# The down projection of pairs 2 and 3 in seven products over all eight pieces, with the last two pieces' sums kept among the token operands

## The reference

```python
xn = layernorm(x)
q, k, v = (xn @ W.T + b for each)              # 512 -> 512
kv_sum = cumsum((elu(k) + 1) * v, axis=1)
s = ((elu(q) + 1) * kv_sum * SCALE) @ Wo.T + bo
y = fwht(xn * SU_ug) / 64                      # Walsh-Hadamard transforms
hid = silu(y @ W_gate.T * ws_gate) * (y @ W_up.T * ws_up)     # 512 -> 2048
g = silu((fwht(hid * SU_dp) / 64) @ W_down.T * ws_down)       # 2048 -> 512
out = x + s * g
```

## Time and profile before

| | us |
|---|---|
| median of 3 runs | 1291.22 (1289.54 to 1293.17) |
| the profiled execution's own time | 1291.18 |
| its span, first to last instruction | 1289.4 |
| PE busy | 1259.5 (98%) |
| DVE busy | 936.1 (73%) |
| ACT busy | 618.3 (48%) |
| POOL busy | 108.9 (8%) |

### The profile page before, as it was taken

One profiled execution on the slowest core, in us unless ns is written; L12 is line 12 of the kernel. 1 busy time (PEld: TensorE's weight loads), 2 busy tenths in 40 slices (PEclk: granted clock), 3 DMA queues, 4 the chain that ended last, 5 costly groups with the idle time before them and its releaser, 6 DMA issues.

```text
span 1289.4 us, 16166 instructions
## 1 busy us (share of the span) xinstructions
PE 1259.5 (98%) x5896; PEld 570.7 (44%) x5896; DVE 936.1 (73%) x1417; ACT 618.3 (48%) x912; POOL 108.9 (8%) x159
## 2 busy tenths in 40 slices
PE   5999999999999999999999999999999999999998
PEld 3544444444444444444444444444444444444443
DVE  6989989878656777777883778776773767775724
ACT  5894655532245655552334555554233655454212
POOL 1000001131210000120022001000001000000001
PEclk9999999999999999999999999999999999999999
DMA  9534775777757356575378333323526433332423
GB/s 370 224 131 125 242 215 186 241 251 292 229 205 237 113 196 231 220 251 196 131 229 257 134 128 134 131 99 103 205 93 196 145 117 116 113 129 76 130 95 103
DMA packets 65472, 226.21 MB, mean 175 GB/s; under 512 B 7408, under 2 KB 17904, under 8 KB 50800
## 3 DMA queue, kind: packets, MB, share of 16 engines
q1 hardware_dynamic: 41840, 170.64, 36.7%
q0 software_dynamic: 16272, 42.48, 11.9%
q10 hardware_dynamic: 7280, 12.06, 2.7%
HBM read 171.64 MB, written 53.50 MB: 175 GB/s over the span
## 4 chain that ended last, share of the span: by engine, by line
PE 78%; DVE 9%; issue 5%; ACT 5%; DMA 3%; SPq 0%; DVEq 0%; ACTq 0%
PE bank L2450 40%; PE bank L2636 13%; PE bank L2330 12%; PE bank L2516 7%; PE bank L2541 2%; PE bank L2661 2%; ACT work L1229 1%; ACT work L1232 1%; DMA h_all<-scr_f 1%; DVE work L1675 1%; PE bank L2375 1%; PE bank L2561 1%; DVE work L1659 1%; DVE work L1665 1%; DVE work L1702 1%
## 5 line engine op out<-in xcount | busy, mean ns | idle before, releaser
L2450 PE MATMUL bank<-xops,ring 128*128 128x512 f16 x2772 | 603.2, 379 | 7.4 <-DVE work L1702 2.6
L2450 PEld LDWEIGHTS bank<-xops,ring 128*128 128x128 f16 x2772 | 269.4, 98 | 340.2 <-issue 11.1
L2330 PE MATMUL bank<-xops,ring 128*128 128x512 f16 x1008 | 225.2, 379 | 0.5 <-DVE ring L1831 0.5
L1212 ACT ACTIVATE work<-bank 128x512 f32<-128x512 f32 x198 | 117.8, 595 | 214.7 <-PE bank L2450 200.2
L1659 DVE TENSOR_TENSOR work<-bank,work 128x512 f32<-128x512 f32 x198 | 133.4, 686 | 113.0 <-PE bank L2450 99.8
L2636 PE MATMUL bank<-h_all,ring 128*128 128x512 f16 x768 | 166.8, 379 | 0.2 <-DVE work L1659 0.2
L2330 PEld LDWEIGHTS bank<-xops,ring 128*128 128x128 f16 x1008 | 98.1, 98 | 123.6 <-issue 9.1
L2636 PEld LDWEIGHTS bank<-h_all,ring 128*128 128x128 f16 x768 | 75.0, 98 | 91.0 <-DVE work L1659 0.7
L1259 ACT ACTIVATE h_all<-work 128x512 f16<-128x512 f32 x116 | 70.6, 624 | 62.6 <-DVE work L1702 62.5
L1711 DVE TENSOR_TENSOR h_all<-work,h_all 128x512 f16<-128x512 f32 x116 | 79.3, 686 | 5.7 <-ACT h_all L1259 4.4
L1665 DVE SCALAR_TENSOR_TENSOR work<-work 128x512 f32<-128x512 f32 x64 | 44.1, 690 | 51.2 <-ACT work L1232 50.8
(11 more groups left out here) (284 smaller groups left out, 1323.4 us busy)
## 6 DMA issues: line engine op xcount, KB each, us to landing
ring<-scr_g SPq DMA_DIRECT2D x72, 1024.0 KB, 4.8
ring<-scr_d SPq DMA_DIRECT2D x15, 1024.0 KB, 5.8
scr_g<-ring SPq DMA_DIRECT2D x22, 512.0 KB, 4.4
h_all<-in_ug_t SPq DMA_DIRECT2D x8, 1024.0 KB, 12.9
ring<-in_down_t SPq DMA_DIRECT2D x6, 1024.0 KB, 6.5
scr_g<-ring POOLq DMA_DIRECT2D x12, 512.0 KB, 5.7
work<-in_x_t SPq DMA_DIRECT2D x6, 1024.0 KB, 7.0
scr_g<-h_all POOLq DMA_DIRECT2D x12, 512.0 KB, 2.9
```

The lines of the kernel that those rows point to most:

```text
L1212: act.activation(tile(g, j), chain_bank(g)[:, :], ACT.Copy).then_inc(copied, 1)
L2330: mm = pe.matmul(plain_bank(g, j)[:, :], at[:, s, 2 * dh + kk, r, :], xops[:, kk, xs, PLAIN_B[dh][c], :], start=(n == 0), stop=(n == len(t ...
L2450: mm = pe.matmul(to[:, :], weight_of(slot, s, b, kk), at, start=(a == 0 and m in (P1, P2, P5)), stop=(a == 5), skip_group_check=True)
```

## The change

SEVEN becomes 8: `seven` goes over all eight pieces, and `rest` goes, with its products, banks, weights and additions. In numbers of instructions for each of the pairs 2 and 3: the down product had 7 x 2 x 18 + 4 x 2 x 12 = 348 matmuls and has 7 x 2 x 24 = 336. The order of its products is now P1, P2, P6, P7, P4, P5, P3, both halves of each in turn, so P1 of the second half now stands ahead of both halves of P2, and P4 ahead of P5.

T2, T3 and T4 of pieces 6 and 7 have no home left; they go to the token operands `xops`, in the places of T2 and T3 (and of B21 for T4), once the last up group has used them (P2 for piece 6, P7 for piece 7). They are written by two instructions, of 1024 and of 512 columns. Pair 3's tokens come into `xops` later, since `x_high(3, 0)` now also waits for P4 of both halves. `load_x(3)` also waits for piece 7's sums. The token preparation of pair 3 on ACT and DVE is cut up and mixed with silus and additions. Two more units (6 and 7) are made in pair 1. There is one weight slot less to load in each pair (seven loads of 1 MB for eight).

In the diff `hidden_sums_high`, `x_high` and the first `seven_and_o` are ACT's, the second `seven_and_o` and `last_sums` DVE's, `seven` is PE's; IN_RES is 6.

```diff
-SEVEN_FROM, SEVEN = 2, 6
-DOWN_SLOTS = (P1, P2, P6, P7, P5, R11, P4, P3)
+SEVEN_FROM, SEVEN = 2, FP
+DOWN_SLOTS = (P1, P2, P6, P7, P4, P5, P3)
+DOWN_ORDER = [(d, m) for m in DOWN_SLOTS for d in range(2)]
-GATE_ORDER = [(d, j) for j in (C11, C22, C21, C12) for d in range(2)]
+GATE_ORDER = [(d, j) for j in (C11, C21, C22, C12) for d in range(2)]
...
+        def homes_late(i, s):
+            b = (T2, T3)[i - IN_RES]
+            return xops[:, :, s, b, :], xops[:, i - IN_RES, s, B21, :]
...
             def load_x(p):
                 sp.wait_ge(h_ready, 32 * p)
+                if p > SEVEN_FROM:
+                    sp.wait_ge(hidden_sums_ready, sums_of_hidden(p - 1, SEVEN - 1))
...
             def load_last_res():
+                sp.wait_ge(seven_done, down_to(PAIRS - 1, 1, P5))
...
             def x_high(p, kk):
                         act.wait_ge(product_done, products_to(p - 1, GROUPS - 1, P3))
+                        act.wait_ge(seven_done, down_to(p - 1, 1, P4))
...
             def hidden_sums_high(p, i):
+                act.wait_ge(product_done, products_to(p, GROUPS - 1, (P2, P7)[i - IN_RES]))
+                two, third = homes_late(i, HI)
+                act.activation(two, work[:, at:at + 2, :], ACT.Copy)
+                act.activation(third, work[:, at + 2, :], ACT.Copy).then_inc(hidden_sums_hi, 1)
...
             def seven_and_o(p):
-                if p < PAIRS - 1:
-                    x_high(p + 1, 0)
-                    t_high(p + 1, 0)
-                    x_high(p + 1, 1)
-                    t_high(p + 1, 1)
                 for d, j in GATE_ORDER:
+                    if p < PAIRS - 1:
+                        if (d, j) == (0, C21):
+                            x_high(p + 1, 0)
+                        elif (d, j) == (0, C22):
+                            t_high(p + 1, 0)
+                            x_high(p + 1, 1)
+                        elif (d, j) == (0, C12):
+                            t_high(p + 1, 1)
                     seven_gate(p, d, j)
...
             def seven_and_o(p):
+                for d in range(2):
+                    seven_add(p, d, "11")
                 if p < PAIRS - 1:
                     x_sums(p + 1, 0)
                     t_low(p + 1, 0)
-                for d in range(2):
-                    seven_add(p, d, "22a")
+                seven_add(p, 0, "22")
                 if p < PAIRS - 1:
-                    x_sums(p + 1, 1)
-                    t_low(p + 1, 1)
-                for d, a in DOWN_SUMS[2:]:
-                    seven_add(p, d, a)
+                    x_adds(p + 1, 1)
+                seven_add(p, 1, "22")
+                if p < PAIRS - 1:
+                    x_low(p + 1, 1)
+                    t_low(p + 1, 1)
+                for d in range(2):
+                    seven_add(p, d, "12")
...
             def last_sums(p):  
                 hidden_low(p, g, C21)
+                if p >= SEVEN_FROM:
+                    for part in range(2):
+                        hidden_sums(p, FP - 1, part)
+                    hidden_sums_low(p, FP - 1)
...
             def seven(p, d, m):
                 if m == P1:
-                    pe.wait_ge(h_ready, 32 * p + 4 * SEVEN)
+                    pe.wait_ge(h_ready, 32 * p + 4 * SEVEN - 3)
                 elif m == P2:
+                    pe.wait_ge(h_ready, 32 * p + 4 * SEVEN - 1)
...
+                elif m == P4:
+                    pe.wait_ge(seven_copied, down_copied_to(p, d, P7))
+                elif m == P3:
+                    pe.wait_ge(seven_summed, down_summed_to(p, d, "22"))
```

More of the change, by code:

```diff
@@ L212, in load_of, with loads_of @@
 def load_of(p, g):
-    return g if g < GROUPS else g + (KB if p < SEVEN_FROM else 2 * KB)
+    return g if g < GROUPS else g + (KB if p < SEVEN_FROM else len(DOWN_SLOTS))
+def loads_of(p):
+    return PIECES + (2 * KB if p < SEVEN_FROM else len(DOWN_SLOTS))
 def slot_of(p, n):
@@ L220, in slot_of @@
         return RING[n % len(RING)]
-    return LATER_RING[(LOADS * (p - SEVEN_FROM) + n) % len(LATER_RING)]
+    return LATER_RING[(loads_of(p) * (p - SEVEN_FROM) + n) % len(LATER_RING)]
 def dmas_of(p, n):
-    return 2 if p >= SEVEN_FROM and GROUPS <= n < GROUPS + 2 * KB else 1
-ALL_LOADS = [(p, n) for p in range(1, PAIRS) for n in range(LOADS)]
+    return 2 if p >= SEVEN_FROM and GROUPS <= n < GROUPS + len(DOWN_SLOTS) else 1
+ALL_LOADS = [(p, n) for p in range(1, PAIRS) for n in range(loads_of(p))]
 def loads_into(p, n):
@@ L764, in load @@
                         sp.wait_ge(piece_stored[s], 16 * len(range(s, GROUPS, 3)))
-                if p >= SEVEN_FROM and GROUPS <= n < GROUPS + 2 * KB:
+                if p >= SEVEN_FROM and GROUPS <= n < GROUPS + len(DOWN_SLOTS):
                     load_seven(p, n)
@@ L768, in load @@
                 if p >= SEVEN_FROM:
-                    piece = n if n < GROUPS else n - 2 * KB
+                    piece = n if n < GROUPS else n - len(DOWN_SLOTS)
                 else:
@@ L866, in _ @@
             for p in range(1, PAIRS):
-                for n in range(LOADS):
+                for n in range(loads_of(p)):
                     load(p, n)
@@ L2480, in group @@
                     for d, m in DOWN_ORDER[1:]:
-                        if m < R11:
-                            seven(p, d, m)
-                        else:
-                            rest(p, d, m)
+                        seven(p, d, m)
                 elif g + 1 == GROUPS:
@@ L2518, in seven @@
                                        stop=(i == SEVEN - 1 and n == 2), skip_group_check=True)
-                mm.then_inc(seven_done, 1)
-            def rest(p, d, m):
-                n = GROUPS + DOWN_SLOTS.index(R11)
-                slot = slot_of(p, n)
-                r, c = {R11: (0, 0), R21: (1, 0), R22: (1, 1), R12: (0, 1)}[m]
-                if m == R11:
-                    pe.wait_ge(slot_loaded[slot], 16 * loads_into(p, n))
-                    pe.wait_ge(h_ready, 32 * p + 4 * FP)
-                elif m == R21:
-                    pe.wait_ge(seven_copied, down_copied_to(p, d, P7))
-                elif m == R12:
-                    pe.wait_ge(seven_summed, down_summed_to(p, d, "22a"))
-                elif p == SEVEN_FROM:
-                    pe.wait_ge(gate_ready, 8 * p)
-                else:
-                    pe.wait_ge(seven_summed, down_summed_to(p - 1, d, "22"))
-                to = {R11: right_bank(d), R21: chain_bank(d), R22: bank[REST_BANKS[d]], R12: left_bank(d)}[m]
-                terms = [(i, half, s, xs) for i in range(SEVEN, FP) for half in range(2)
-                         for s, xs in ((HI, HI), (HI, LO), (LO, HI))]
-                for n, (i, half, s, xs) in enumerate(terms):
-                    mm = pe.matmul(to[:, :], rest_weight(slot, half, d + 2 * r, i, s), h[:, i, 2 * half + c, xs, :],
-                                   start=(m == R22 and n == 0), stop=(n == len(terms) - 1), skip_group_check=True)
                 mm.then_inc(seven_done, 1)
```

71 lines of the change are left out of this document (38 added, 33 removed).

## The result

| | before | changed |
|---|---|---|
| median us | 1291.16 (1289.54 to 1293.17) | 1302.92 (1300.53 to 1303.79) |
| profiled execution's own time | 1291.18 | 1303.79 |
| its span | 1289.4 | 1302.0 |
| its mean granted TensorE clock | 1.000 | 0.993 |

A forecast was written before the change was run, and what follows sets the result against it. PE, busy 98% of the span, was taken to bound the kernel. Against 1291.18: pair 1 0, pair 2 -2.59 + 3.76 + 4.3 - 0.5 = +5.0, pair 3 -2.59 + 3.76 = +1.2; in all +6.2, 1297.4 us, range 1292.5 to 1300.5.

The forecast's parts named there:

- The 12 matmuls less in each pair: Down product of pairs 2 and 3: 348 to 336 matmuls, 2.59 us less a pair, 5.18 us in all.
- The wait before P1: Down product, both pairs: PE waits for DVE's first LO part of piece 7, 3.76 us each, bounds 2.99 and 4.5.
- The wait before P3 in pair 2: Down product, pair 2: PE waits 4.3 us for the addition to x_res, where it was 0.5; bounds 0 and 5.8.
- No wait before P3 in pair 3: Down product, pair 3: no tokens to prepare, so the addition is ready in time; no wait.
- none before P6: Down product: piece 7's own sums, some 8 us, are hidden behind 72 matmuls, 15.5 us; no wait.
- pair 1 free: Pair 1: two more units delay silus by 4.6 us, but the fourth waits for PE anyway; cost 0.
- No stop of PE in the down product is put down to a DMA: Loads and queues: the later load_x(3), P4's load and load_last_res have over 20 us to spare; costed at nothing.
- the term for what follows a stop: Matmuls behind the new stops before P1 and P3: pitch taken as whole, extra cost 0.
- rival (c): New stops before P1 and P3 also slow matmuls behind them, 2.6 us a loss: one gives 1300.0, three 1305.2; chance 0.08.
- the sign by which the prediction called itself wrong: Wrong if P1 has no wait, P3's is under 2 us, or matmuls behind a stop come 0.43 us apart.
- rival (b): Down product: DVE and ACT run ahead of PE and cover the waits before P1 and P3; 1285.5 us; chance 0.04.

The follow-up runs named there:

- e7: The kernel before, with units 6 and 7 also made and stored in pair 1 and read by nobody; 1290.35 us, ratio 0.9993.
- e6: The kernel before, with only P1 of the down product made to wait for piece 7's first LO part, which it doesn't read; 1300.13 us, ratio 1.0063.
- e2: The changed kernel, with DVE's addition of C22, first half, moved ahead of pair 3's token preparation; 1296.15 us, ratio 1.0045.
- e3: The changed kernel, with P1's wait moved to piece 7's own matmuls and the C22 addition moved ahead of the tokens; 1285.57 us, ratio 0.9957.
- e1_wait_at_use: The changed kernel, with P1's wait for piece 7 moved from ahead of the half product to piece 7's three matmuls; 1290.85 us, ratio 0.9999.
- e5_tail_first: The changed kernel, with the last up group's P4 and P3 (12 matmuls) put ahead of the first P1 half; 1293.20 us, ratio 1.0014.
- e8_half_filled: The changed kernel, with 7 unused matmuls ahead of each of the same three waits, P1 in both pairs and P3 in pair 2; 1298.39 us, ratio 1.0055.
- e4_filled: The changed kernel, with unused matmuls ahead of three waits: 14 before P1 in both pairs, 15 before P3 in pair 2; 1296.84 us, ratio 1.0045.

## Why the prediction failed

**The 12 matmuls less in each pair** were right: L2553 has x384 in one group where all go by h_all, the whole line 672, and the pitch was 0.216 wherever PE had not stopped.

**The wait before P1** was right in both pairs, in place, releaser and size: 3.80 and 3.79 from start to start against 3.76. The chain on DVE went step for step. Its timeline of the changed kernel, to be held against the earlier trace rows:

```profile
890.13 1.23 DVE L1757 TENSOR_TENSOR xops<-work,xops 128x1024 f16<-128x1024 f32 x1 [0.32 <-ACT xops L1283]
891.27 0.68 DVE L1758 TENSOR_TENSOR xops<-work,xops 128x512 f16<-128x512 f32 x1
891.88 0.68 DVE L1679 TENSOR_TENSOR work<-bank,work 128x512 f32<-128x512 f32 x1
...
893.91 0.69 DVE L1731 TENSOR_TENSOR h_all<-work,h_all 128x512 f16<-128x512 f32 x1
```

DVE waits for ACT's second instruction into xops, then has 1024 and 512 columns ahead of P5's addition, as written. The LO part starts at 893.91 against 893.62, in a pair that starts 0.46 earlier, so 0.75 later; the forecast was 0.76.

**The wait before P3 in pair 2** was right in place and releaser and near in size: 4.02 against 4.3. DVE's timeline, to be held against the earlier trace rows:

```profile
956.73 1.28 DVE L2106 TENSOR_TENSOR h_all<-bank,h_all 128x512 f32<-128x512 f32 x2
...
963.30 2.36 DVE L1663 TENSOR_TENSOR xops<-work,xops 128x1024 f16<-128x1024 f32 x2 [0.89 <-ACT xops L1070]
965.58 0.68 DVE L2106 TENSOR_TENSOR x_res<-bank,x_res 128x512 f32<-128x512 f32 x1
```

From the start of the two additions to that of the x_res addition it is 8.85 us (956.73 to 965.58); forecast were 24.3 - 15.19 = 9.1. E, the first matmul behind P7, is 941.68 in PE's timeline above, which puts the addition at E + 23.9 for a forecast of 24.3.

**No wait before P3 in pair 3, none before P6, and pair 1 free** were right; pair 1 was by 0.46 better than free, since e7 shows the load in time again. The last silus there ran later than written (from 690.22, not 688.7) and still in time. No stop of PE in the down product is put down to a DMA, as forecast.

**The step that failed** is the term for what follows a stop, the one that took the pitch behind a stop of 3.8 or 4.3 us to be whole. The prediction had seen both ends, with a stop of 0.50 us and no loss, with 14.58 us and 2.6 us lost, and placed its stops in between at the cheap end. There was no ground for that: the chance of 0.08 for rival (c) was a guess, where rows spoke for both, and the range let in one loss on top of the middle of the forecast, not three and not one on top of its upper bound. What came is rival (c), with matmuls behind the stops 0.43 us apart, the sign by which the prediction called itself wrong: at that distance 5 us hold some 12 and a part of one at either end, and the stretch from 895 to 900 has 13. Its price was about right: 2.6 a loss, measured 1.57 to 2.94; three losses were to give 1305.2, and it became 1302.9. As a term of the sum it stood at 0 and was 7.4 us.

The prediction's reading that the page grants the full clock in every slice said more than the page does, as a 9 there is 90% or more. For the first transposes the finer view has a granted clock of 1.00 as well, from 14.58 us on, so that row showed a loss behind a stop and not its cause; the clock's part is shown by the rows of the changed kernel and of e6. The Trainium skill's rule that stood beside rival (c) (TensorE: Matmul & The Clock Gate, HAM oscillation — how this bites in real kernels), that idle gaps between bursts can put the array back to half clock and that the next burst begins at 1.2 GHz, agrees with the changed kernel's trace: 0.50 from 895 to 900 us. It doesn't hold for every stop: in e6 and in e2's pair 2 the clock was still whole when the matmuls began again, and fell 0.5 to 1.3 us later, and behind e2's stop of 3.63 us in pair 3 it didn't fall.

**Why rival (b), the faster side, did not come,** though the change as such holds it: e3 reaches its 1285.5 with 1285.57. (That the two agree to a tenth is luck: 0.46 us gained in pair 1 and 0.6 lost at a new stop were not in the sum.) Seven products over eight pieces are worth their 5.2 us. The change lost them by two placements, the wait for the last piece at the first matmul of a product, and the addition for the next product behind preparations for the next pair.

## What to carry over

A wait of the engine that bounds belongs ahead of the first instruction that needs the data, not ahead of the product it is in. Of a sum over pieces the newest comes last, and its wait with it. On the helping engine, what PE's next product waits for goes ahead of what only the next stage needs. And by these runs a stop of TensorE of some 3 to 4 us is priced at its length and up to 3 us more, for the slow matmuls behind it; where it can't be removed, unused matmuls in it can be the faster choice.

## What the hardware showed that was not expected

What a stop lost to the clock, in the profiled executions. The third column gives from when to when the granted clock was 0.50, read from stretches of 0.25 us, and the fourth how long after the stop's end that was still so:

| kernel, place | idle us | clock at 0.50, us from the start | of it behind the stop, us | lost, us |
|---|---|---|---|---|
| changed, P1 of pair 2 | 3.63 | 893.9 to 900.7 | 6.0 | 2.94 |
| changed, P1 of pair 3 | 3.63 | 1201.1 to 1204.5 | 3.2 | 1.57 |
| changed, P3 | 3.85 | 965.5 to 972.4 | 6.0 | 2.93 |
| e2_add_first, P1 of pair 2 | 3.63 | 895.1 to 898.5 | 3.4 | 1.68 |
| e2_add_first, P1 of pair 3 | 3.63 | never | 0 | 0 |
| e1_wait_at_use, P3 | 3.85 | 959.7 to 963.1 | 3.1 | 1.49 |
| e5_tail_first, P3 | 3.85 | 958.6 to 965.4 | 5.0 | 2.46 |
| e6_wait_alone, P1 of pair 2 | 2.88 | 895.4 to 898.8 | 3.4 | 1.69 |
| e6_wait_alone, P1 of pair 3 | 2.88 | 1195.8 to 1199.2 | 3.4 | 1.69 |
| e8_half_filled, three stops | 2.08, 2.25, 2.08 | never | 0 | 0, 0, 0 |
| e4_filled, three stops | 0.56, 0.52, 0.57 | never | 0 | 0, 0, 0 |

The same stop, of the same length and with the same instructions on both sides, loses anything from 0 to 2.9 us. In every row the loss is half of the time that matmuls spent at 0.50, within 0.1 us, so the clock accounts for all of it. The clock fell up to 1.8 us before a stop ended or up to 1.3 us after. What decides when it falls, how long it stays down, and whether it falls at all, stays open.

The other surprise is in pair 1. From 685 to 700 us POOL's loads of the tokens into x_res took a median of 14.5 us to land in the changed kernel and 4.3 before, since it had more to store, while the ring's weight loads took 9.0 instead of 10.3, and PE's wait for one of them went away. e7, which adds the two units to the kernel before and nothing else, has 13.7 and 9.1 there, so the units do it. That the later loads of POOL made room for the weights fits these numbers, but was not tested by itself.
